# One step of a fused LSTM, attention, GRU and mixture-of-experts kernel laid out in another order

## The chip, the cores and the metric

The kernel runs on one core of a Trainium2 chip. The metric is the device time of one execution in microseconds (us). TensorE is called PE, VectorE DVE, ScalarE ACT, GpSimd POOL.

## The reference

Input x is 16 sequences of 128 time steps and 128 features. The result is x plus attention over an LSTM's output, and to that is added a mixture of experts over a GRU's output:

```python
x = x + attention(lstm(x, cond))      # causal softmax, 16 heads, rank-32 latents
x = x + experts(gru(x, cond))         # 8 experts of 512, top 2 of 8 by softmax

# LSTM step                           # GRU step
a = xw_t + h @ Wh                     z, r = sigmoid(comb @ Wz + bz), sigmoid(comb @ Wr + br)
c = f * c + i * g                     cand = tanh(concat(x_t, r * h) @ Wh + bh)
h = o * tanh(c)                       h = (1 - z) * h + z * cand
                                      # after every fourth step: h = tanh(h @ Wp + bp)
# experts
h = gelu(x @ w1 + b1); out_all = h @ w2 + b2     # exact gelu
out = sum of the two selected experts' rows, by their renormalised weights
```

Both recurrences are serial in time, 128 steps each. The attention is causal over time, so a block of 16 time steps can be attended to as soon as the LSTM has passed it. The GRU follows 29 steps behind the LSTM.

## The kernel before

The whole program is one loop over steps k, written out for each engine by hand. Step k holds LSTM step t = k and GRU step g = k - 29 (`LAG`), so both recurrences run in steps 29 to 127, only the LSTM before, only the GRU up to step 156, and after it what is left of the experts. Everything else is hung into fixed steps by their place modulo 16, which is called the phase below. Every engine works through its queue in the order in which the code stands, and semaphores tie the queues together.

In a step PE issues `g_step` (the two GRU gates into pG), `l_step` (four LSTM gates into pL), `g_candidate` (needs gRZ from DVE), and at the end of every fourth step `g_propagate`. ACT does tanh of each into gT, lT, gC, then lC, the tanh of the LSTM's cell. DVE makes gRZ and gA from gT, lP, oK and the cell (written to lT) from lT, then gB, ghi, g and glo (the GRU's new state, its high half and its low half), and hhi, hfull, hlo (the same for the LSTM). `l_fill` and `g_fill` put eight steps' input projections into pL and pG at once.

The attention of a block of 16 times is a visit of 8 units, each with two batch rows: `scores` at phase `O_S` plus the unit's number (13 small matmuls into pS, a single bank), then DVE's `maximum` (mx) and `subtract` (P), ACT's `exps` in place, `turn_probs` (transposes P into pV) at `O_T`, ACT's `pt_copy` (PTs), `values` at `O_V`, DVE's `normalise` and `turn_values`. `project` at two phases (`O_P`) closes each half block. `lat_q` makes latents and queries of 8 time steps. POOL spreads the queries into qbd.

The experts' visit m covers 16 GRU steps in two token tiles of 128 (tg 0 and 1). `expert_up(m, e, cp)` is 6 matmuls into pH[cp], one bank for each half cp of the hidden columns; ACT's `activate` (gelu) empties it into hid, two instructions for each cp. `expert_down(m, e, tg)` is a bias matmul and 4 fp32 matmuls into pY, and DVE's `combine` adds it to acc. Each down waits for the combine of the one before it. Routing is `route_x` on PE, `route_first` on DVE, a tanh (th) on ACT in the same step, and `route_rest` (10 small DVE instructions) one step later. `keep_warm(n)` issues n matmuls of 512 columns on zeros: 4 a step before step 18, 2 a step up to step 44. Two queue orders matter most:

```python
if route_at(k) is not None:                       # ACT, end of step k
    act.wait_ge(r_low, 2 * m + tg + 1)
    A(th[:, :], low[:, :], ACT.Tanh, scale=0.5).then_inc(r_th, 1)
...
if n >= 2:                                        # PE, expert_up
    pe.wait_ge(gelu, 2 * (n - 1))                 # the same bank's gelu of the expert before
```

Of the kernel before, what the change touches and what calls it, by code (L numbers as in the profile page):

```python
# [8 lines left out]
GS = 8  # L9
# [13 lines left out]

LAG = 29
O_S, O_T, O_V = 2, 3, 4
O_P = (9, 12)
O_R = (5, 13)
LAST = T + LAG
E_STEP = (0, 0, 1, 2, 2, 3, 4, 4)
NHID = 8  # L30
WARM_END = LAG + TB
W1_STEP = (17, 18, 19, 20, 21, 22, 23, 25)
# [15 lines left out]
def route_at(k):  # L48
    for tg, o in enumerate(O_R):
        q, r = divmod(k - o, TB)  # L50
        if r == 0 and 2 <= q <= NBLK + 1:
            return q - 2, tg
    return None


def up_at(k):
    out = []
    for m in range(NBLK):
        for e in range(E):
            at = LAST + e if m == NBLK - 1 else TB * m + LAG + TB + E_STEP[e]  # L60
            if at == k:
                out += [(m, e, 0), (m, e, 1)]
    return out


def down_at(k):
    out = []
    for m in range(NBLK):
        for e in range(E):
            for tg in range(2):  # L70
                at = LAST + 1 + e if m == NBLK - 1 else TB * m + LAG + TB + 2 + 2 * e + tg
                if at == k:
                    out.append((m, e, tg))
    return out


STEPS = LAST + 1 + E


def build(nc, a, out):  # L80
# [8 lines left out]
    with ctx:  # L89
# [179 lines left out]
        sub_done = sem("sub_done")  # L269
# [46 lines left out]
        def _(sp):  # L316
# [20 lines left out]
            for m in range(NBLK):  # L337
                for tg in range(2):
                    sp.wait_ge(acc_done, 2 * (E * m + E - 1) + tg + 1)
                    row = (2 + 2 * m + tg) * TOK  # L340
                    sp.dma_start(out[row:row + TOK, :], acc[:, m % 3, tg, :]).then_inc(stored[2 * (m % 3) + tg], 16)
            for m in range(NBLK - 3, NBLK):
                for tg in range(2):
                    sp.wait_ge(stored[2 * (m % 3) + tg], 16 * (m // 3 + 1))

        @block.gpsimd
        def _(pool):
# [41 lines left out]
            def rank_experts(m, tg):  # L389
                n = 2 * m + tg  # L390
                pool.wait_ge(r_cmp, 2 * n + 1)
                pool.tensor_tensor(eq[:, :, :], eq[:, :, :], tri[:, :, :], ALU.mult).then_inc(r_rank, 1)  # L392
                pool.wait_ge(r_cmp, 2 * n + 2)
                pool.wait_ge(r_rank, 2 * n + 1)
                pool.tensor_tensor(gt[:, :, :], gt[:, :, :], eq[:, :, :], ALU.add).then_inc(r_rank, 1)
                pool.wait_ge(r_rank, 2 * n + 2)

            for k in range(STEPS):
                if k % GS == 0 and GS <= k <= T:
                    split_latents(k // GS - 1)  # L400
# [5 lines left out]
                if route_at(k) is not None:  # L406
                    rank_experts(*route_at(k))

        @block.tensor
        def _(pe):  # L410
# [18 lines left out]
            def before_c(k):  # L429
                nq = len([j for j in range(k) if j % GS == 0 and GS <= j <= T])  # L430
                npj = len([j for j in range(k) if half_at(j) is not None])
                nr = len([j for j in range(k) if route_at(j) is not None])
# [27 lines left out]
            def lat_q(G, k):  # L460
                hi, lo = (flat(t[:, GS * G + 1:GS * G + GS + 1, :]) for t in (hhi, hlo))
                pe.wait_ge(l_lo, GS * G + GS)
                if G == 0:
                    pe.wait_ge(set_kvd, 2)
                    pe.wait_ge(set_qk, 1)
                    pe.wait_ge(set_qklo, 1)
                if G:
                    pe.wait_ge(lat_done, G)
                before = len([j for j in range(k) if unit_at(j, O_S) is not None])
                if before:  # L470
                    pe.wait_ge(sub_done, before)
                mm(pS[:, 0:TOK], Wkvdhi[:, :], hi, start=True)
                mm(pS[:, 0:TOK], Wkvdhi[:, :], lo)
                mm(pS[:, 0:TOK], Wkvdlo[:, :], hi).then_inc(lat_mm, 1)
# [8 lines left out]
            def scores(n, k):  # L483
# [6 lines left out]
                pe.wait_ge(lat_done, min(k // GS, NG))  # L490
                if n:
                    pe.wait_ge(sub_done, n)
# [9 lines left out]
            def turn_probs(n):  # L502
                pe.wait_ge(exp_done, n + 1)
# [543 lines left out]
```

## Time and profile before

| | |
|---|---|
| three runs | 729.1, 722.74, 728.73 us (median 728.73) |
| profiled execution | 724.37 us, of it 722.6 us span |
| PE, DVE, ACT, POOL busy | 86%, 58%, 41%, 19% |
| PE's granted clock, mean | 0.898 |
| chain that ended last | PE 64%, DVE 18%, ACT 10%, issue 6% |

PE is the engine that is most busy, but its matmuls overlap and their ends are modelled, so 86% does not say that PE is full; the chain says for what share of the time something else was what the end waited for. The clock tells what share of full speed (2.4 GHz) PE was granted; 1.2 GHz shows as 0.5.

### The profile page before, as it was taken

How to read it: one execution, taken by the hardware profiler on the slowest of the kernel's cores; microseconds unless marked ns; L12 is line 12 of the kernel's file. 1: busy time of each engine (PE TensorE's matmuls, PEld its weight loads, DVE VectorE, ACT ScalarE, POOL GpSimd, SP SyncE). 2: the span in 40 equal slices, each digit the busy share in tenths (PEclk: the TensorE clock that was granted, in tenths of full speed). 3: DMA queues.
4: the chain of work that ended last, by engine and by line, in shares of the span. 5: the costliest groups of instructions: out<-in, count | busy, mean ns of one | idle time of the engine just before them, and what ended most of it. 6: DMA issues, size and time to landing. Idle time of an engine off the chain costs nothing.

```text
span 722.6 us, 18818 instructions
## 1 busy us (share of the span) xinstructions
PE 623.3 (86%) x6952; PEld 550.6 (76%) x6952; DVE 420.9 (58%) x2372; ACT 293.4 (41%) x1004; POOL 134.3 (19%) x339
## 2 busy tenths in 40 slices
PE   5988889988899888898898889888988888877898
PEld 2656767876788878887888778877888688766787
DVE  2476656664586558655776478655875476435321
ACT  1354323235532464245422653355434532451143
POOL 4006204200331024102320043003310231000000
PEclk8795785599988999999979999999999999998599
DMA  9400000000000000000000000000000000000000
GB/s 257 176 1 1 2 1 1 3 1 1 2 3 1 5 5 3 2 5 5 3 1 2 8 3 3 1 10 1 2 2 5 6 1 2 4 6 2 0 8 9
DMA packets 5528, 10.03 MB, mean 14 GB/s; under 512 B 1827, under 2 KB 4527, under 8 KB 5054
## 3 DMA queue, kind: packets, MB, share of 16 engines
q1 hardware_dynamic: 4686, 6.47, 2.5%
q10 hardware_dynamic: 752, 2.37, 1.3%
q8 instruction: 56, 0.92, 0.6%
q14 instruction: 34, 0.28, 0.1%
HBM read 7.79 MB, written 1.05 MB: 12 GB/s over the span
## 4 chain that ended last, share of the span: by engine, by line
PE 64%; DVE 18%; ACT 10%; issue 6%; DMA 1%; SPq 0%; POOL 0%; DVEq 0%; POOLq 0%
PE pY L412 18%; PE pG L412 11%; PE pH L412 10%; PE pV L412 8%; PE pL L412 6%; PE pV L507 4%; ACT hid L746 4%; PE pS L412 3%; PE pC L412 3%; ACT PTs L736 2%; DVE acc L940 1%; DMA lWx<-in_lWx 1%; DVE gRZ L949 1%; DVE ghi L965 1%; DVE mx L858 1%
## 5 line engine op out<-in xcount | busy, mean ns | idle before, releaser
L412 PE MATMUL pY<-w,hid 128*128 128x128 f32 x1024 | 155.3, 299 | 0.0
L412 PEld LDWEIGHTS pY<-w,hid 128*128 128x128 f32 x1024 | 136.3, 207 | 0.1
L746 ACT ACTIVATE hid<-pH,b 128x256 f32<-128x256 f32 x256 | 105.6, 471 | 63.0 <-PE pH L412 61.6
L385 POOL COPY qbd<-qh 32x256 f16<-32x256 f16 x256 | 104.3, 408 | 141.5 <-PE pS L412 127.8
L949 DVE SCALAR_TENSOR_TENSOR gRZ<-gT,g 128x32 f32<-128x32 f32 x128 | 26.8, 210 | 115.4 <-ACT gT L754 115.2
L412 PE MATMUL pG<-gRZ,gW 128*128 128x16 f32 x256 | 51.1, 276 | 36.5 <-DVE gRZ L949 36.4
L412 PE MATMUL pV<-latN,PTs 128*128 128x33 f32 x512 | 76.8, 298 | 6.6 <-ACT PTs L736 6.6
L736 ACT ACTIVATE PTs<-pV 128x512 f32<-128x512 f32 x64 | 38.2, 597 | 107.6 <-PE pV L507 107.6
L412 PEld LDWEIGHTS pG<-gRZ,gW 128*128 128x128 f32 x256 | 42.8, 210 | 46.1 <-DVE gRZ L949 45.3
L412 PEld LDWEIGHTS pV<-latN,PTs 128*128 128x128 f32 x512 | 70.1, 212 | 9.4 <-ACT PTs L736 8.6
L412 PE MATMUL pH<-ghi,w1hi 128*128 128x256 f16 x256 | 70.6, 276 | 6.6 <-ACT hid L746 5.5
L412 PE MATMUL pH<-glo,w1hi 128*128 128x256 f16 x256 | 70.8, 277 | 0.0
L412 PE MATMUL pH<-ghi,w1lo 128*128 128x256 f16 x256 | 70.7, 276 | 0.0
L940 DVE SCALAR_TENSOR_TENSOR acc<-pY,gates,acc 128x128 f32<-128x128 f32 x128 | 44.4, 347 | 33.6 <-PE pY L412 32.4
L962 DVE TENSOR_TENSOR gB<-gRZ,gC 128x16 f32<-128x16 f32 x128 | 24.2, 189 | 61.6 <-ACT gC L764 60.9
L764 ACT ACTIVATE gC<-pG 128x16 f32<-128x16 f32 x128 | 23.3, 182 | 81.8 <-PE pG L412 81.6
L754 ACT ACTIVATE gT<-pG 128x32 f32<-128x32 f32 x128 | 24.8, 194 | 70.5 <-PE pG L412 70.5
L412 PE MATMUL pY<-still 128*128 128x512 bf16 x138 | 48.8, 476 | 1.2 <-DVE still L786 1.2
L392 POOL TENSOR_TENSOR eq<-eq,tri 128x64 f32<-128x64 f32 x16 | 5.1, 318 | 238.1 <-DVE gt L904 238.1
L507 PE MATMUL pV<-ident,P 128*128 128x128 f32 x256 | 46.5, 312 | 2.5 <-DVE On L874 2.5
L412 PE MATMUL pL<-hhi,lWhi 128*128 128x16 f16 x512 | 41.8, 171 | 4.4 <-DVE hhi L969 4.4
L412 PEld LDWEIGHTS pL<-hhi,lWhi 128*128 128x128 f16 x512 | 35.2, 102 | 13.1 <-DVE hhi L969 11.0
(155 smaller groups left out, 1448.3 us busy)
## 6 DMA issues: line engine op xcount, KB each, us to landing
w<-in_w SPq DMA_DIRECT2D x2, 2048.0 KB, 10.8
out<-acc SPq DMA_DIRECT2D x16, 64.0 KB, 1.5
xT<-in_xT ACTq DMA_DIRECT2D x1, 960.0 KB, 10.4
hid<-in_WqT ACTq DMA_DIRECT2D x1, 512.0 KB, 5.6
hid<-in_Wout ACTq DMA_DIRECT2D x1, 512.0 KB, 7.9
lWh<-in_lWh SPq DMA_DIRECT2D x1, 256.0 KB, 2.8
lWx<-in_lWx SPq DMA_DIRECT2D x1, 256.0 KB, 9.5
gWh<-in_gWh SPq DMA_DIRECT2D x1, 192.0 KB, 7.5
```

The costliest lines, as they stand in the source:

```text
L385: pool.tensor_copy(qbd[r, n % 2, :, :, q, :], qh[r, p % 2, :, 2 * u:2 * u + 2, :, :].rearrange("p l b (g c) t -> p l (b g) (c t)", g=2)).t ...
L412: return nc.tensor.matmul(o, lhsT=lhsT, rhs=rhs, start=start, stop=stop, skip_group_check=True)
L507: last = nc.tensor.transpose(pV[:, 128 * j:128 * (j + 1)], P[:, n % 3, j, :], ident[:, :])
L736: A(PTs[:, n % 2, :, :].rearrange("p j q -> p (j q)"), pV[:, :], ACT.Copy).then_inc(pt_done, 1)
L746: A(hid[:, e % NHID, 2 * cp + c, :], pH[cp][:, 256 * c:256 * (c + 1)], ACT.Gelu, bias=b1[:, e, 2 * cp + c:2 * cp + c + 1], scale=1.0 / SP) ...
L754: A(gT[:, :, :], pG[:, 0:2, g % GS, :], ACT.Tanh, scale=1.0 / SP).then_inc(g_tanh, 1)
L764: A(gC[:, :], pG[:, 2, g % GS, :], ACT.Tanh, scale=1.0 / SP).then_inc(g_c, 1)
L858: V.tensor_reduce(mx[:, :], S_of(keys(n // NU)), AX.X, ALU.max).then_inc(mx_done, 1)
L940: V.scalar_tensor_tensor(acc[:, m % 3, tg, :], pY[:, D * tg:D * (tg + 1)], gates[:, m % 2, tg, e:e + 1], acc[:, m % 3, tg, :], ALU.mult, A ...
L949: V.scalar_tensor_tensor(gRZ[:, :, :], gT[:, :, :], 1.0, g8[:, at:last + 1:last - at, :], ALU.add, ALU.mult).then_inc(g_rh, 1)
L962: V.tensor_tensor(gB[:, :], gRZ[:, 1, :], gC[:, :], ALU.mult).then_inc(g_b, 1)
L965: V.scalar_tensor_tensor(ghi[:, g, :], gA[:, :], keep, gB[:, :], ALU.mult, ALU.add).then_inc(g_hi, 1)
```

## The change

- The step's order. PE now issues `g_step`, a first slot of other work (A: `values`, the second `project`, `lat_q` at phase 0, a down), `g_candidate`, then `l_step`, then a second slot (B) with everything else, and `scores` last of all. ACT and DVE follow: lT, lC, lP, oK and the cell come behind gC and behind glo.
- The exp. `subtract` is gone; `maximum` gives the negated maximum and moves one step later, ahead of gB. The exp reads pS directly with the maximum as its bias, one instruction for each of the four blocks, two of them ahead of lC and two behind it. `O_S` goes from 2 to 1, and the next unit's scores wait for all four exps, where they waited for the subtraction.
- The experts. Visits now cover tiles 2m-1 and 2m, so there are nine, the first and the last of one tile. Up matmuls are one expert a step at phases 10 to 15, 0 and 1, both cp in the step, and their gelus follow one step later, cp 0 between gT and gC, cp 1 behind lC. Downs stand in the table `DOWNS`, up to three in a group with one wait for the group.
- The routing on DVE is cut in four (`route_first`, `route_soft`, `route_pick`, `route_gates`, the last three 2, 3 and 4 steps after `route_x`), and ACT's th moves to the end of the following step.
- `keep_warm` writes to pH[1], with 4 a step up to step 28 and 2 + 2 a step in 29 to 41. Latents go to a quarter of pY, not to pS.

```diff
-O_S, O_T, O_V = 2, 3, 4
+O_S, O_T, O_V = 1, 3, 4
-E_STEP = (0, 0, 1, 2, 2, 3, 4, 4)
-WARM_END = LAG + TB
+NVIS = NBLK + 1
+WARM_END = 42
+TAIL = 149
+UPS = tuple(42 + e for e in range(E))
+DOWNS = ((45, "A", (0, 0)), (46, "A", (0, 1)), (47, "A", (1, 0)), (49, "A", (1, 1)), (49, "B", (2, 0)),
...
+def up_step(m, e):
+    return LAST + e if m == NVIS - 1 else TB * NBLK + 37 - TB + e if m == NVIS - 2 else TB * m + UPS[e]
...
             def scores(n):
-                    pe.wait_ge(sub_done, n)
+                    pe.wait_ge(exp_done, 4 * n)
...
+            def experts_down(group):
+                for at, (m, e, tg) in enumerate(group):
+                    n = ORDER[(m, e, tg)]
+                    pe.wait_ge(gelu, 4 * (E * m + e + 1))
...
+                    elif at == 0:
+                        pe.wait_ge(acc_done, n)
...
             for k in range(STEPS):      # PE
                 if 0 <= g < T:
                     g_step(g)
+                if unit_at(k, O_V) is not None:
+                    values(unit_at(k, O_V))
+                if half_at(k) is not None and k % TB == O_P[1]:
+                    project(half_at(k), k)
+                if latents_at(k) is not None and k % TB == 0:
+                    lat_q(latents_at(k), k)
+                if (k, "A") in DOWN_AT:
+                    experts_down(DOWN_AT[(k, "A")])
+                if LAG <= k < WARM_END:
+                    keep_warm(k, 2)
+                if 0 <= g < T:
+                    g_candidate(g)
                 if t < T:
                     l_step(t)
...
+                for m, e in UP_AT.get(k, []):
+                    expert_up(m, e, 0)
...
+                for m, e in UP_AT.get(k, []):
+                    expert_up(m, e, 1)
...
+                if unit_at(k, O_S) is not None:
+                    scores(unit_at(k, O_S))
+                if k < WARM_END:
+                    keep_warm(k, 0 if k in (1, 2) else 2 if k >= LAG else 4)
...
+            def exps(n, pair):          # ACT
+                act.wait_ge(mx_done, n + 1)
+                for j in (2 * pair, 2 * pair + 1):
+                    A(P[:, n % 3, j, 0:L], S_of(L)[:, j, :], ACT.Exp, bias=mx[:, j:j + 1]).then_inc(exp_done, 1)
...
+                for m, e in UP_AT.get(k - 1, []):
+                    activate(m, e, 0)
                 if 0 <= g < T:
                     act.wait_ge(g_cand, g + 1)
...
+                if unit_at(k - 1, O_S) is not None:
+                    exps(unit_at(k - 1, O_S), 0)
...
+                if unit_at(k - 1, O_S) is not None:
+                    exps(unit_at(k - 1, O_S), 1)
+                for m, e in UP_AT.get(k - 1, []):
+                    activate(m, e, 1)
```

ACT's queue where an attention visit begins. Before, one load of the exp's table (L730) stands ahead of the first exp, between lT and gC:

```order
L754 ACTIVATE gT<-pG 128x32
L757 ACTIVATE lT<-pL 128x64
L730 ACT_TABLE_LOAD
L730 ACTIVATE P<-P 128x4x64
L764 ACTIVATE gC<-pG 128x16
L767 ACTIVATE lC<-lT 128x16
```

Now, in steps of phase 2 and 3, with the last expert's gelu (hid) between the exps (P):

```order
L781 ACT_TABLE_LOAD
L781 ACTIVATE P<-pS,mx 128x64 x2
L818 ACTIVATE lC<-lT 128x16
L781 ACTIVATE P<-pS,mx 128x64 x2
L798 ACT_TABLE_LOAD
L798 ACTIVATE hid<-pH,b 128x256 x2
L805 ACTIVATE gT<-pG 128x32
L810 ACTIVATE gC<-pG 128x16
L813 ACTIVATE lT<-pL 128x64
L781 ACT_TABLE_LOAD
L781 ACTIVATE P<-pS,mx 128x64 x2
```

There are two loads more in each visit that overlaps an expert visit: 26 in the program where there were 14.

DVE's queue in a step of phase 5 (attention in full course). Before, the LSTM's cell (lP, oK, lT) stood ahead of the normalisation (rs, On) and of the GRU's update (gB to glo):

```order
L949 SCALAR_TENSOR_TENSOR gRZ<-gT,g 128x32
L951 SCALAR_TENSOR_TENSOR gA<-gT,g 128x16
L954 SCALAR_TENSOR_TENSOR lP<-lT 128x32
L955 TENSOR_SCALAR oK<-lT 128x16
L957 SCALAR_TENSOR_TENSOR lT<-lP 128x16
L872 RECIPROCAL rs<-pV 128x4
L874 TENSOR_TENSOR On<-pV,rs 128x128
L962 TENSOR_TENSOR gB<-gRZ,gC 128x16
L965 SCALAR_TENSOR_TENSOR ghi<-gA,gB 128x16
L966 SCALAR_TENSOR_TENSOR g<-gA,gB 128x16
L969 TENSOR_TENSOR hhi<-oK,lC 128x16
```

Now the combine (acc) and the maximum (mx) of the step before come ahead of gB, and the cell comes behind all of them:

```order
L1003 SCALAR_TENSOR_TENSOR gA<-gT,g 128x16
L992 SCALAR_TENSOR_TENSOR acc<-pY,gates,acc 128x128
L913 TENSOR_REDUCE mx<-pS 128x4
L1010 TENSOR_TENSOR gB<-gRZ,gC 128x16
L1013 SCALAR_TENSOR_TENSOR ghi<-gA,gB 128x16
L1014 SCALAR_TENSOR_TENSOR g<-gA,gB 128x16
L1016 TENSOR_TENSOR glo<-g,ghi 128x16
L917 RECIPROCAL rs<-pV 128x4
L919 TENSOR_TENSOR On<-pV,rs 128x128
L1023 SCALAR_TENSOR_TENSOR lP<-lT 128x32
L1024 TENSOR_SCALAR oK<-lT 128x16
L1026 SCALAR_TENSOR_TENSOR lT<-lP 128x16
```

The cell, on which ACT's lC waits, moved from the fifth place in the step to the thirteenth.

## Rows read from the trace of the kernel before

**Rows 1.** Stretches: length; busy PE, PEld, DVE, ACT, POOL; granted clock; DMA.

```profile
55.90:99.00 43.10, 37.87 (x401) 31.57 (x402) 26.25 (x122) 15.19 (x47) 14.49 (x31) 0.72 0.01 2
99.00:166.90 67.90, 61.55 (x638) 51.05 (x635) 41.26 (x261) 19.75 (x87) 14.83 (x38) 0.67 0.01 2
166.90:259.40 92.50, 81.71 (x992) 74.21 (x989) 55.80 (x346) 45.24 (x156) 16.21 (x42) 0.93 0.01 3
259.40:335.60 76.20, 66.08 (x853) 61.37 (x849) 49.38 (x293) 34.45 (x123) 15.41 (x40) 0.98 0.01 4
335.60:626.10 290.50, 253.17 (x3028) 236.07 (x3025) 189.05 (x1034) 125.81 (x427) 60.14 (x156) 0.96 0.01 3
626.10:682.60 56.50, 44.69 (x365) 39.93 (x362) 22.97 (x137) 19.85 (x68) 1.27 (x4) 0.82 0.01 4
682.60:722.60 40.00, 34.23 (x272) 30.24 (x272) 10.24 (x42) 13.89 (x35) 0.64 (x2) 0.92 0.03 8
```

**Rows 2.** Groups by line and form, 259.4 to 335.6 us: busy, mean ns.

```profile
L746 ACT ACTIVATE hid<-pH,b 128x256 f32<-128x256 f32 x32 | 13.2, 472 | 6.3 <-PE pH L412 6.0
...
L940 DVE SCALAR_TENSOR_TENSOR acc<-pY,gates,acc 128x128 f32<-128x128 f32 x16 | 5.5, 346 | 0.1
...
L757 ACT ACTIVATE lT<-pL 128x64 f32<-128x64 f32 x16 | 3.6, 225 | 0.9
...
L867 DVE TENSOR_TENSOR P<-pS,mx 128x256 f32<-128x256 f32 x8 | 3.4, 424 | 0.3
...
L858 DVE TENSOR_REDUCE mx<-pS 128x4 f32<-128x256 f32 x8 | 3.3, 413 | 0.0
```

**Rows 3.** Timeline of step 147, GRU only: start, length, engine, line.

```profile
652.18 0.20 ACT L754 ACTIVATE gT<-pG 128x32 f32<-128x32 f32 x1 [1.01 <-PE pG L412]
...
652.66 0.39 PE L412 MATMUL pG<-gRZ,gW 128*128 128x16 f32 x2 [0.51 <-DVE gRZ L949]
...
653.09 0.18 ACT L764 ACTIVATE gC<-pG 128x16 f32<-128x16 f32 x1 [0.71 <-PE pG L412]
653.31 0.18 DVE L962 TENSOR_TENSOR gB<-gRZ,gC 128x16 f32<-128x16 f32 x1 [0.62 <-ACT gC L764]
...
653.81 0.17 DVE L973 TENSOR_TENSOR glo<-g,ghi 128x16 f16<-128x16 f32 x1
...
654.29 0.20 ACT L754 ACTIVATE gT<-pG 128x32 f32<-128x32 f32 x1 [1.01 <-PE pG L412]
```

**Rows 4.** Timeline of ACT in step 77, phase 13: a table load before gelu.

```profile
320.66 1.28 ACT L746 ACT_TABLE_LOAD   x1
...
321.96 0.84 ACT L746 ACTIVATE hid<-pH,b 128x256 f32<-128x256 f32 x2
...
322.69 0.18 ACT L764 ACTIVATE gC<-pG 128x16 f32<-128x16 f32 x1
```

**Rows 5.** The chain of waits in order of time: pieces of steps 68 and 69.

```profile
277.98 0.39 PE pS L412 x13
...
282.00 0.93 PE pV L412 x8
```

**Rows 6.** The chain of waits at the end: ups (x6) and downs (x9).

```profile
709.97 0.66 PE pH L412 x6
710.62 1.04 PE pY L412 x9
...
720.21 0.35 DVE acc L940
```

**Rows 7.** Timeline at the end of step 69: ACT's th, and gT behind it.

```profile
286.64 0.21 ACT L778 ACTIVATE th<-low 128x8 f32<-128x8 f32 x1 [1.05 <-DVE low L906]
...
286.76 0.18 ACT L754 ACTIVATE gT<-pG 128x32 f32<-128x32 f32 x1
```

**Rows 8.** Timeline of step 67: DVE beside POOL's copies.

```profile
274.46 1.81 POOL L385 COPY qbd<-qh 32x256 f16<-32x256 f16 x4 [1.33 <-PE pS L412]
...
274.91 0.41 DVE L962 TENSOR_TENSOR gB<-gRZ,gC 128x16 f32<-128x16 f32 x1 [1.03 <-ACT gC L764]
```

More of the change, by code:

```diff
@@ L335, in _ @@
                 sp.dma_start(whole(t), a[name]).then_inc(loaded_moe, 16)
-            for m in range(NBLK):
-                for tg in range(2):
[L339 to L344, printed above, removed]
+            for i in range(NG):
+                m, tg = visit_of(i)
+                sp.wait_ge(acc_done, ORDER[(m, E - 1, tg)] + 1)
+                row = (2 + i) * TOK
+                sp.dma_start(out[row:row + TOK, :], acc[:, m % 3, tg, :]).then_inc(stored[2 * (m % 3) + tg], 16)
+            for m in range(NVIS - 3, NVIS):
+                for tg in range(2):
+                    used = slots_used(m, tg) + (tg < len(tiles_of(m)))
+                    if used:
+                        sp.wait_ge(stored[2 * (m % 3) + tg], 16 * used)
         @block.gpsimd
@@ L398, in _ @@
             for k in range(STEPS):
-                if k % GS == 0 and GS <= k <= T:
-                    split_latents(k // GS - 1)
+                if latents_at(k) is not None:
+                    split_latents(latents_at(k))
                 n = unit_at(k, O_S)
@@ L429, in before_c @@
             def before_c(k):
-                nq = len([j for j in range(k) if j % GS == 0 and GS <= j <= T])
+                nq = len([j for j in range(k) if latents_at(j) is not None])
                 npj = len([j for j in range(k) if half_at(j) is not None])
-                nr = len([j for j in range(k) if route_at(j) is not None])
+                nr = len([j for j in range(k) if j in ROUTES])
                 bank_c(nq, npj, nr)
@@ L466, in lat_q @@
                     pe.wait_ge(set_qklo, 1)
+                n = len([d for (at, slot), ds in DOWN_AT.items() if at < k for d in ds])
                 if G:
                     pe.wait_ge(lat_done, G)
[L469 to L474, printed above, removed]
+                if n:
+                    pe.wait_ge(acc_done, n)
+                M = pY[:, 3 * TOK:4 * TOK]
+                mm(M, Wkvdhi[:, :], hi, start=True)
+                mm(M, Wkvdhi[:, :], lo)
+                mm(M, Wkvdlo[:, :], hi).then_inc(lat_mm, 1)
                 before_c(k)
@@ L481, in lat_q, with scores @@
                 last.then_inc(q_mm, 1)
-            def scores(n, k):
+            def scores(n):
                 p, u = divmod(n, NU)
@@ L620, in _ @@
-                if 0 <= g < T:
-                    g_candidate(g)
-                if k % GS == 0 and GS <= k <= T:
-                    lat_q(k // GS - 1, k)
-                if unit_at(k, O_S) is not None:
-                    scores(unit_at(k, O_S), k)
-                while ups or downs:
-                    if downs:
-                        expert_down(*downs.pop(0))
-                    if ups:
-                        expert_up(*ups.pop(0))
                 if unit_at(k, O_T) is not None:
@@ L781, in _ @@
                     A(gp, pG[:, 3, (g + 1) % GS, :], ACT.Tanh, scale=1.0 / SP).then_inc(g_p, 1)
+                if unit_at(k, O_T) is not None:
+                    pt_copy(unit_at(k, O_T))
+                if latents_at(k) is not None:
+                    q_copy(latents_at(k))
+                if k - 1 in ROUTES:
+                    n = ROUTES[k - 1]
+                    act.wait_ge(r_low, n + 1)
+                    A(th[:, :], low[:, :], ACT.Tanh, scale=0.5).then_inc(r_th, 1)
         @block.vector
```

307 lines of the change are left out of this document (156 added, 151 removed).

## The prediction, made before the changed kernel was run

> **What bounds the kernel now.** I read the stretches first [rows 1], then one bare step [rows 3], then the single pieces. Between 166.9 and 626.1 us lie steps 45 to 140, 96 steps in 459.2 us (92.5 + 76.2 + 290.5), so 76.5 us for 16 steps or 4.8 a step; that is where the time is. A step with only the GRU and one down takes 2.11 us from gT to gT [rows 3], and PE's own work in 16 steps comes to about 61 us from the pieces: an expert with both tiles is 2 x 0.66 up and 2 x 1.0 down, so 26.6 for eight; a unit 0.39 for scores, 0.93 for values [rows 5] and 0.45 for transposes, so 14.2 for eight; the recurrences' own matmuls about 0.7 a step, 11; latents, projections and fills about 9. So some 15 of 76 us are latency: an engine's queue stands behind an instruction that waits. PE "busy" 66.1 of 76.2 [rows 1] hides this. The question is not how much work is left but which waits each step holds in the new order.
>
> **Unit costs.** From the bare step [rows 3], with gT's start as 0: the candidate's matmul at 0.48, gC 0.43 after it, gB 0.22 after gC, glo 0.50 after gB, and the next gT 0.48 after glo (0.35 after the first matmul of `g_step`). DVE's small instructions start 0.1 apart where independent and 0.2 where one feeds the next. A pair of gelus is 0.84 (two of 0.47 overlapping [rows 2, 4]). A table load is 1.28, and the gelu starts 0.02 behind it [rows 4].
>
> **A step with experts (phases 11 to 15, 0, 1), new order.** The down in slot A ends 0.75 after gT, so the candidate is at 0.75, gC 1.18, gB 1.40, glo 1.90, lP 2.0, cell 2.2, lC 2.4. Only then comes gelu cp 1, 2.5 to 3.35. Up cp 1 of the next expert uses the same bank and waits: 3.5 to 4.15 (0.66 [rows 6]). `g_step` is queued behind it: gT at 4.5. So 4.5 us for one expert a step, PE idle about 1.2 of it. Phase 15 adds `l_fill` behind that up (a 512-column bias and four fp32 matmuls, about 1.1 at a down's 0.24 each [rows 6]): 5.6. Phases 12 and 0 have the propagation, whose next gate matmuls are fp32 (+0.3), and an early wait for x1: 5.05 and 4.7. Phase 1 adds scores 0.4 and a down that waits for its combine: 5.1. Phase 11 has the table load ahead of gelu cp 0, and so ahead of gC: 6.05.
>
> **A step with attention (phases 4 to 8).** Values end 0.7 after gT, gC 1.15, gB 1.37 (combine 0.35 and maximum 0.41 [rows 2] are over by 1.1, so they are hidden), glo 1.87, rs and On to 2.46, cell 2.6, lC 2.8, second exp pair 2.9 to 3.43, scores 3.55 to 3.9, gT 4.26. Adding the exps: an exp of 64 from PSUM without a bias would be as lT, 0.225; with one it goes by gelu's 0.472 for 256 [rows 2], less 192 elements at the 0.83 ns that 64 to 256 cost at least, 0.31. I take 0.31, since gelu also carries a bias pointer; the pair is 0.53, and the low end 0.35 would save 0.18 in each of seven steps. What goes is the subtraction, 0.424 on DVE [rows 2], but it lay where DVE had time. Results: phase 4 is PE's own 4.7 (with `g_fill`), 5 to 7 are 4.3, 8 is 4.6, and 9 and 10 (q_rest and routing push gRZ late, `pt_copy` pushes values) 4.7 and 4.6.
>
> The Trainium skill, ScalarE: Activation LUTs, What ACT_TABLE_LOAD costs, gives an ACTIVATE with a bias pointer as 280 ns and 0.833 ns an element, 0.33 for 64. The gelu row, 0.472 against 0.493 by that rule, agrees within 5%; the sum would be longer by 0.3 us in 16 steps.
>
> **The loads.** The queue order shows two more a visit. Phase 2: gT, gelus, gC, lT to 1.3, load to 2.6, exps, lC 3.0, exps to 3.7, load to 5.0, gelu cp 1 to 5.8, gT 5.7 where the same phase took 2.6 before. Phase 3: its load runs while DVE does three combines and the maximum, the exps wait for it, 4.65. Twelve loads more are 15.4 us on ACT at 1.28 [rows 4]; about 2.5 of each visit's 2.6 ends up in the steps' length.
>
> The same section of the Trainium skill gives 1283 ns for the load and 1380 ns for a drain, 2.66 us a switch, and its rule is to batch calls by set, which speaks against this change. The load's row agrees, the drain's does not: the gelu starts 0.02 us after the load's end. By the page twelve switches would be 31.9 us, by the row 15.4.
>
> **What improves.** ACT's th stood directly ahead of gT [rows 7], with the whole routing on DVE ahead of it; it cost about 0.8 us twice in 16 steps. Two experts in one step with a load (phase 13, 5.9 us before) becomes 4.5. Phases 5 to 7 gain up to 1 us each.
>
> **The sum for 16 steps.** Phases 0 to 15: 4.7, 5.1, 5.7, 4.65, 4.7, 4.3, 4.3, 4.3, 4.6, 4.7, 4.6, 6.05, 5.05, 4.5, 4.5, 5.6 = 77.3. The same count on six phases of before (3, 4, 5, 10, 11, 12) gives 24.5 where the trace has 25.7, because DVE stretches beside POOL's copies (gB 0.41 for 0.18 [rows 8]) and semaphores take time; with that 5% it is 81.2. Before has 77.1 for the five such periods (steps 45 to 124) and 73.6 for the sixth, of which the most is without the LSTM.
>
> **The whole, against the profiled span of 722.6:**
> - Steps 0 to 17: same chain, 0.
> - Steps 18 to 28, 43.1 us at clock 0.72 [rows 1]: the two further warm-up matmuls keep it high, as four did before step 18; a step is then about 3.9 (values 0.93, l_step and lT 0.5, lC 0.7, exps and scores 1, warm-up 0.86) for 4.7. Sum 37: -6. If the clock stays low, +7 instead.
> - Steps 29 to 44, 67.9 us at 0.67: high clock, but the LSTM's half of DVE now runs behind the GRU's, and four warm-up matmuls (0.86) lie on the path: 70, +2.
> - Five periods: 5 x (81.2 - 77.1) = +20.5; longer key rows with the block's number +5 (before holds them already); the first expert visit has one tile, -7. Sixth period 70 for 73.6, -4. Together +15.
> - Steps 141 to 155: 57 for 56.5 (626.1 to 682.6), +1.
> - After: 40.0 us before, 16 downs at 0.66 + 1.04 each [rows 6] behind the routing of the last tiles. Now the last visit has one tile: step 156 3.9, three grouped steps 3, 3 and 4.1, seven experts at 1.7, and 2.4 to the end: 28.4, -11.5.
>
> Sum -6 + 2 + 15 + 1 - 11.5 = +0.5: a span of 723, a time of 725. That execution lies below the median of the three (724.4 and 728.7), so I say **724 us**, the change a trade that comes out about even.
>
> **The rivals.**
> - Faster: the new order's waits overlap better than a chain worked out step by step says (gelu cp 1 slips ahead, exps at 0.35 a pair, no stretch beside POOL), so that a period comes near 75. Then 6 x 6 less: 724 - 36 = 688, and with half of it 706. For it: PE's own 61 us, and the balance of the phases, 3.0 to 4.7 of PE's work in each. Against: lC is last on a queue of DVE that I cannot shorten, and before, the same count was too short, not too long. Chance 0.33, at 680 to 714.
> - Slower: the exps as gate of the recurrence. Scores of a unit wait for the exps behind lC and `g_step` is queued behind the scores, so in seven steps of 16 every stretch on DVE between gRZ and the cell (13 instructions) is on the path. If they stretch like gB [rows 8] in half of the cases, that is 0.6 a step, 4.2 a period, 25 in all: 749. It decides from a phase 5 of over 4.9 us. For it: POOL's copies fall in just these phases (15.4 us of 76.2 [rows 1]). Chance 0.22, at 736 to 760.
> - The clock: PE idles 1.2 us in most steps and the granted clock falls more often than before (0.93 to 0.98 in this stretch [rows 1]). 30 us more at 1.2 GHz cost about 12: 736. Chance 0.1.
> - Forecast 0.35, at 714 to 736.
>
> **How the numbers follow.** Within 1% is about what a measurement of this kernel can tell from no change: 721.4 to 736.0 by the median. Of the forecast's 0.35 some 0.09 lie below and 0.01 above. Faster 0.33 + 0.09 = 0.42; the same 0.25 and a few hundredths of the clock's case, 0.28; slower the rest, 0.30. The range that leaves out 2 in 10 is 690 to 750; the forecast's own is 714 to 736.
>
> **What would show it.** Phases 13 and 14 at 4.5 us with up cp 1 waiting for the gelu; phase 2 near 5.7 with 26 loads in all; phases 5 to 7 at 4.3 to 4.6, scores waiting for exp; phase 11 over 5.5; after the last gT 28 us; clock near 1 in steps 18 to 44. I am wrong if phases 11 to 15 run below 4 us (then the gelu is not the gate) or if phases 4 to 8 run above 5.

## Result and profile after

| | before | after |
|---|---|---|
| median, lowest to highest | 728.91 us (722.74 to 732.34) | 855.91 us (853.5 to 860.1) |
| profiled execution, its span | 724.37, 722.6 us | 853.5, 851.6 us |
| PE's granted clock, mean | 0.898 | 0.836 |

The change makes the kernel 17.6% slower: the ratio is 1.176 [1.167, 1.185]. Forecast were 724 us and a range of 690 to 750. Totals go by medians; the profiled executions of the kernels in experiments 1, 6 and 9 ran longer (806 us for 794, 773 for 767, 771 for 749) and at a lower clock than their other runs.

The page of the changed kernel: busy time, the granted clock in 40 slices, shares of the chain, and two groups (busy, mean ns, then PE's idle time in front of them and what ended it).

```profile
PE 679.1 (80%) x7090; PEld 603.3 (71%) x7090; DVE 398.2 (47%) x2308; ACT 354.2 (42%) x1240; POOL 131.5 (15%) x339
...
PEclk8886966665667998789977998789977998599999
...
PE 63%; DVE 16%; ACT 13%; issue 6%; DMA 1%; SPq 0%; POOL 0%; DVEq 0%; POOLq 0%; ACTq 0%
...
L538 PE MATMUL pV<-ident,P 128*128 128x128 f32 x256 | 59.8, 378 | 68.1 <-DVE On L919 66.4
...
L443 PE MATMUL pH<-ghi,w1hi 128*128 128x256 f16 (+1 forms) x288 | 77.1, 273 | 43.5 <-ACT hid L798 42.7
```

The same two groups before, in the view by line:

```profile
L412 PE MATMUL pH<-ghi,w1hi 128*128 128x256 f16 x256 | 70.6, 276 | 6.6 <-ACT hid L746 5.5
...
L507 PE MATMUL pV<-ident,P 128*128 128x128 f32 x256 | 46.5, 312 | 2.5 <-DVE On L874 2.5
```

The chain's shares have hardly moved. What has moved are two of PE's waits: the transposes of P stood 2.5 us behind DVE's On, now 66.4, and the ups 5.5 us behind the gelu, now 42.7. Besides, the transposes take 378 ns for 312, a sign of the clock.

The stretches after (length; busy PE, PEld, DVE, ACT, POOL; clock; DMA), for [rows 1]: steps 18 to 28, 29 to 44, 45 to 124, 141 to 155 and the rest; behind them phases 5 to 11 of steps 64 to 79 alone.

```profile
60.20:105.20 45.00, 39.33 (x404) 30.07 (x404) 22.78 (x112) 18.45 (x72) 9.38 (x25) 0.78 0.01 2
105.20:192.50 87.30, 70.40 (x691) 56.94 (x690) 39.24 (x253) 28.31 (x121) 14.86 (x38) 0.67 0.01 1
192.50:669.40 476.90, 377.00 (x4150) 353.26 (x4150) 238.07 (x1417) 212.87 (x741) 77.04 (x200) 0.84 0.01 3
760.40:822.20 61.80, 52.45 (x493) 47.37 (x491) 24.60 (x146) 23.78 (x83) 1.33 (x4) 1.00 0.01 2
822.20:851.60 29.40, 24.36 (x258) 23.05 (x257) 8.53 (x39) 12.74 (x43) 0.64 (x2) 1.00 0.04 11
...
330.60:378.10 47.50, 38.72 (x378) 36.54 (x379) 22.89 (x137) 16.82 (x63) 5.79 (x15) 0.75 0.01 3
```

Before, steps 45 to 124 took 385.6 us at a clock of 0.96; now they take 476.9 at 0.84. Of 129.0 us more of span, 91 are there, 19 in steps 29 to 44 and 17 in steps 125 to 140.

Step 69 (phase 5), which the forecast put at 4.3 us and which takes 6.19:

```profile
330.59 0.20 ACT L805 ACTIVATE gT<-pG 128x32 f32<-128x32 f32 x1 [0.22 <-PE pG L443]
...
331.76 0.24 PE L443 MATMUL pL<-hlo,lWhi 128*128 128x16 f16 x4
...
332.78 0.29 DVE L919 TENSOR_TENSOR On<-pV,rs 128x128 f32<-128x128 f32 x1
...
333.21 1.09 PE L538 MATMUL pV<-ident,P 128*128 128x128 f32 x4 [1.20 <-DVE On L919]
333.41 0.22 ACT L818 ACTIVATE lC<-lT 128x16 f32<-128x16 f32 x1 [0.73 <-DVE lT L1026]
...
334.20 2.02 PE L443 MATMUL pY<-w,hid 128*128 128x128 f32 x8
...
336.78 0.20 ACT L805 ACTIVATE gT<-pG 128x32 f32<-128x32 f32 x1 [1.84 <-PE pG L443]
```

`turn_probs` waits for `on_done`, because the transposes write to pV, the bank in which `values` left what On reads. Before, the transposes came late in PE's step. Now they stand directly behind `l_step`, and On stands on DVE behind combine, maximum and gB to glo. PE stops for 1.20 us, and the down, the scores and the next `g_step` stop with it. Then the down takes 2.02 us, against 1.04 [rows 6]: PE is at 1.2 GHz from 332.7 to 336.1. The LSTM's lC is long done by then, so what the forecast took for the path, glo to cell to lC to the exps, is not what the end of this step waits for.

### The profile page after: what moved, and what is told of

The parts are those of the page before. It is cut to its first block, busy times and chain, and to the rows that moved or that the text cites. A ratio compares the mean times of both kernels' runs of the same rounds, so it can differ in the third digit from the quotient of the medians.

```text
span 851.6 us, 19294 instructions
## 1 busy us (share of the span) xinstructions
PE 679.1 (80%) x7090; PEld 603.3 (71%) x7090; DVE 398.2 (47%) x2308; ACT 354.2 (42%) x1240; POOL 131.5 (15%) x339
## 4 chain that ended last, share of the span: by engine, by line
PE 63%; DVE 16%; ACT 13%; issue 6%; DMA 1%; SPq 0%; POOL 0%; DVEq 0%; POOLq 0%; ACTq 0%
PE pY L443 16%; PE pH L443 13%; PE pG L443 9%; PE pV L538 7%; PE pV L443 6%; ACT hid L798 5%; PE pL L443 5%; PE pC L443 5%; PE pS L443 4%; DVE gB L1010 2%; DVE On L919 2%; ACT L798 2%; ACT gC L810 2%; DVE ghi L1013 2%; DVE glo L1016 2%
## 5 line engine op out<-in xcount | busy, mean ns | idle before, releaser
L443 PEld LDWEIGHTS pY<-w,hid 128*128 128x128 f32 x1024 | 146.5, 220 | 2.3
L798 ACT ACTIVATE hid<-pH,b 128x256 f32<-128x256 f32 (+1 forms) x288 | 111.9, 445 | 12.0 <-PE pH L443 11.8
L538 PE MATMUL pV<-ident,P 128*128 128x128 f32 x256 | 59.8, 378 | 68.1 <-DVE On L919 66.4
L443 PE MATMUL pH<-ghi,w1hi 128*128 128x256 f16 (+1 forms) x288 | 77.1, 273 | 43.5 <-ACT hid L798 42.7
L538 PEld LDWEIGHTS pV<-ident,P 128*128 128x128 f32 x256 | 39.1, 190 | 71.9 <-ACT P L781 59.4
L443 PE MATMUL pH<-ghi,w1lo 128*128 128x256 f16 (+1 forms) x288 | 78.0, 276 | 0.0
L443 PE MATMUL pH<-glo,w1hi 128*128 128x256 f16 (+1 forms) x288 | 77.9, 276 | 0.0
L443 PEld LDWEIGHTS pH<-ghi,w1hi 128*128 128x128 f16 x288 | 29.9, 104 | 53.3 <-issue 49.6
L781 ACT ACTIVATE P<-pS,mx 128x16 f32<-128x16 f32 (+7 forms) x256 | 66.0, 315 | 1.2 <-DVE mx L913 0.6
L818 ACT ACTIVATE lC<-lT 128x16 f32<-128x16 f32 x128 | 27.6, 216 | 90.3 <-DVE lT L1026 89.3
```

What stands on the lines that cost most here:

```text
L443: return nc.tensor.matmul(o, lhsT=lhsT, rhs=rhs, start=start, stop=stop, skip_group_check=True)
L538: last = nc.tensor.transpose(pV[:, 128 * j:128 * (j + 1)], P[:, n % 3, j, :], ident[:, :])
L781: A(P[:, n % 3, j, 0:L], S_of(L)[:, j, :], ACT.Exp, bias=mx[:, j:j + 1]).then_inc(exp_done, 1)
L798: A(hid[:, e % NHID, 2 * cp + c, 0:W], pH[cp][:, 256 * c:256 * c + W], ACT.Gelu, bias=b1[:, e, 2 * cp + c:2 * cp + c + 1], scale=1.0 / SP) ...
L818: A(lC[:, :], lT[:, 4, :], ACT.Tanh, scale=0.5).then_inc(l_tc, 1)
```

## Experiments

Times are medians. The kernel before took 731 to 734 us beside these runs and 728.9 beside the changed kernel, which was not run again, so differences to its 855.9 are uncertain by some 5 us. "Half clock" is the time at 1.2 GHz in steps 45 to 124 of the profiled execution: 34 us before, 157 after.

**1. The transposes moved back behind the downs.** Changed kernel, PE's queue only.

```diff
-                if unit_at(k, O_T) is not None:
-                    turn_probs(unit_at(k, O_T))
                 for m, e in UP_AT.get(k, []):
 ...
                     experts_down(DOWN_AT[(k, "B")])
+                if unit_at(k, O_T) is not None:
+                    turn_probs(unit_at(k, O_T))
```

> The changed kernel with one move: the four transposes of P stand on PE behind the downs of slot B instead of directly behind l_step. Theory A: the transposes wait for On (1.2 to 1.4 us of PE standing still in each step of phases 4 to 10), everything in slot B is queued behind them, and the idle stretch also lets the granted clock fall, so that the down behind it takes 1.9 us for 1.0. Then both go: phases 5 to 7 fall from 6.2 - 6.9 us to 4.3 - 4.9, the granted clock in these phases is near 1, and the time is 770 to 790 us for 856. Rival B: the clock is low for another reason (PE stands still behind the gelus as well), and only the wait's own 0.5 us a step goes: 825 to 840 us. Rival C: transposes that come later make pt_copy and the next step's values late, and nothing is gained.

Measured: 793.6 us (785.1 to 806.3), ratio to before 1.079 [1.070, 1.089], so 62 us less than the changed kernel, a little short of theory A's 770 to 790. Step 69:

```profile
314.45 0.20 ACT L805 ACTIVATE gT<-pG 128x32 f32<-128x32 f32 x1 [0.22 <-PE pG L443]
...
315.78 1.11 PE L443 MATMUL pY<-w,hid 128*128 128x128 f32 x8
...
317.07 0.63 PE L538 MATMUL pV<-ident,P 128*128 128x128 f32 x4 [0.18 <-DVE On L919]
...
318.75 0.20 ACT L805 ACTIVATE gT<-pG 128x32 f32<-128x32 f32 x1 [0.37 <-PE pG L443]
```

The down covers the wait for On, the clock is at 2.4 GHz, and the step takes 4.29 us, the 4.3 of the forecast. Steps 18 to 28 take 39.9 us. But PE's wait for On is 20.8 us in all, phases 7 to 10 still run at half clock in part (4.4 to 8.1 us a step), and half clock is 144 us in the profiled execution. So most of the wait goes here, but from step 64 on only phases 5 and 6 are free of half clock throughout.

**2. On moved ahead of gB.** The same wait, taken from its other end: PE's queue as in the changed kernel, on DVE the normalisation behind the maximum.

```diff
                     maximum(unit_at(k - 1, O_S))
+                if unit_at(k, O_V) is not None:
+                    normalise(unit_at(k, O_V))
 ...
-                if unit_at(k, O_V) is not None:
-                    normalise(unit_at(k, O_V))
```

> The changed kernel with one thing moved on DVE: rs and On (the normalisation) stand behind the maximum and ahead of gB, where they stood behind glo. PE's queue is untouched: the transposes still stand directly behind l_step. It is the same wait as in the kernel with the transposes moved behind the downs (793.6 us), taken from its other end. Theory (the transposes wait for On, and the clock falls with the stall): in a step of phase 5 the values end about 0.9 us after gT, rs and On then take 0.45, so On is over at about 1.5 in place of 2.5 and the transposes wait 0.2 to 0.4 us in place of 1.2; gB comes 0.1 to 0.3 later. Phases 5 to 8 fall from 6.2 to 6.9 us to 4.5 to 5, half clock in steps 45 to 124 falls below 100 us from 157, and the whole is at 785 to 815. Rival 1 (it was not the wait but the place: the gain of the moved transposes came from the downs going ahead of them): the time stays within 10 us of 856. Rival 2 (gB behind On is on the recurrence's path and the clock stays low): 840 to 870, with PE's wait on On gone from the chain but phases 5 to 8 above 6.

Measured: 767.8 us (762.3 to 768.1), 1.047 [1.039, 1.055]: 88 us less than the changed kernel, more than the theory's 785 to 815. Both rivals fall. Step 69, then the wait by line, then phases 5 to 11:

```profile
308.06 0.20 ACT L805 ACTIVATE gT<-pG 128x32 f32<-128x32 f32 x1 [0.22 <-PE pG L443]
...
309.34 0.29 DVE L919 TENSOR_TENSOR On<-pV,rs 128x128 f32<-128x128 f32 x1
...
309.78 0.63 PE L538 MATMUL pV<-ident,P 128*128 128x128 f32 x4 [0.30 <-DVE On L919]
...
310.30 1.11 PE L443 MATMUL pY<-w,hid 128*128 128x128 f32 x8
```

```profile
L538 PE MATMUL pV<-ident,P 128*128 128x128 f32 x256 | 46.1, 309 | 20.2 <-DVE On L919 16.6 <-ACT P L781 3.5
```

```profile
308.06:340.03 31.97, 28.18 (x376) 26.76 (x378) 22.47 (x137) 16.07 (x62) 5.89 (x15) 1.00 0.01 4
```

The wait is 16.6 us for 66.4, the down is back at 1.11 for 2.02, phases 5 to 8 take 4.0 to 4.8 us from step 64 on (but for one of 5.7, at half clock), and the seven phases 5 to 11 take 32.0 us at 2.4 GHz where they took 47.5 at 0.75. Half clock is 68 us. That gB comes later costs nothing that shows. PE's wait is 50 us shorter, and 88 us came back. Which part of them is the clock's, this experiment can't say, since wait and clock went together.

**3. The wait kept, PE kept busy in it.** Changed kernel, five matmuls of 512 columns on zeros ahead of the transposes in phases 4 to 10 (the wait on gelu keeps them off a bank in use).

```diff
                 if unit_at(k, O_T) is not None:
+                    if k % TB > O_T and k >= 52:
+                        pe.wait_ge(gelu, 4 * E * min((k - 42) // TB + (1 if (k - 42) % TB >= 8 else 0), NVIS - 2))
+                        keep_warm(k, 5)
                     turn_probs(unit_at(k, O_T))
```

> The changed kernel with five matmuls of 512 columns on zeros (0.216 us each at full clock, 1.1 together) ahead of the transposes in phases 4 to 10, from step 52 on. The wait for On stays, only PE is busy while it lasts. If the idle stretch is what brings the clock down (theory A), the clock in these phases stays near 1 and phases 5 to 7 fall from 6.2 - 6.9 us to about 4.8 - 5.2; the time is 795 to 815 us. If the clock does not depend on it (B), the ten half-clock matmuls' worth of 2.2 us per step is longer than the wait, and the kernel gets slower by about 0.8 us in 40 steps: 885 us or more.

Measured: 798.8 us (795.5 to 802.7), 1.091 [1.083, 1.098], 57 us less, with more work in the queue and On where it was. Step 69, then the same seven phases:

```profile
323.99 0.20 ACT L808 ACTIVATE gT<-pG 128x32 f32<-128x32 f32 x1 [0.22 <-PE pG L443]
...
325.26 1.24 PE L443 MATMUL pH<-still 128*128 128x512 bf16 x5
...
326.61 0.63 PE L538 MATMUL pV<-ident,P 128*128 128x128 f32 x4
...
327.13 1.11 PE L443 MATMUL pY<-w,hid 128*128 128x128 f32 x8
```

```profile
324.00:361.80 37.80, 34.42 (x407) 28.72 (x408) 22.88 (x137) 16.36 (x62) 5.78 (x15) 1.00 0.01 3
```

The transposes start 2.62 us behind gT, exactly as in the changed kernel, but they take 0.63 us for 1.09 and the down 1.11 for 2.02, so the step takes 4.80 us for 6.19. The seven phases take 37.8 us at 1.00, for 47.5 at 0.75 in the changed kernel and 32.0 with the wait gone: of those 15.5 us, 9.7 come with the clock and the other 5.8 with the wait and whatever the filler adds. Half clock is 48 us. This shows the clock's part as a cause of its own, and that PE's idle time in the stall brings it about.

**4. The loads.** Ups one step earlier: 14 table loads where the changed kernel has 26. Then the same together with experiment 1.

```diff
-UPS = tuple(42 + e for e in range(E))
+UPS = tuple(41 + e for e in range(E))
```

> The changed kernel with the ups of every visit but the last two one step earlier (phases 9 to 0 instead of 10 to 1), so that the last gelu is done before the first exp: 14 table loads for 26. If the two loads a visit are what phases 2 and 3 pay (5.8 and 4.6 to 6.0 us), phase 2 falls to about 4.3 and the time by 15 to 25 us, to 832 to 841. If they lie under the downs anyway, no change: 850 to 860.

> Both edits, transposes behind the downs and ups one step earlier. If the two causes are independent the savings add: theory A gives 750 to 772 us, B 810 to 825. A rest of 20 us or more above the kernel before (729) then belongs to the gelu of the second bank, which comes behind lC and holds back the next up and g_step (phases 13 and 14 at 4.46 us for 4.65 on average over the two before).

Measured: 851.5 us (848.1 to 866.9), 1.162 [1.151, 1.174]; with experiment 1, 789.2 (788.0 to 791.3), 1.078 [1.071, 1.084]. That is 4 us each time (beside the changed kernel, within the 5 us of uncertainty), not 15 to 25. Phase 2 does fall in two periods of five (4.8 and 4.9 us for 5.9), but takes 6.4 to 7.5 in the other three, at half clock, and phase 9, which now holds an up behind a stall at half clock, rises to 8.1 to 9.4 from 6.6 to 7.1. So I had the price of the loads right at their place and wrong in sum. Phase 2 of the changed kernel, as forecast:

```profile
314.99 0.22 ACT L813 ACTIVATE lT<-pL 128x64 f32<-128x64 f32 x1
315.23 1.28 ACT L781 ACT_TABLE_LOAD   x1
316.52 0.52 ACT L781 ACTIVATE P<-pS,mx 128x64 f32<-128x64 f32 x2
316.93 0.21 ACT L818 ACTIVATE lC<-lT 128x16 f32<-128x16 f32 x1
...
317.57 1.28 ACT L798 ACT_TABLE_LOAD   x1
318.86 0.84 ACT L798 ACTIVATE hid<-pH,b 128x256 f32<-128x256 f32 x2
319.59 0.20 ACT L805 ACTIVATE gT<-pG 128x32 f32<-128x32 f32 x1
```

**5. The gelu of cp 1 ahead of lC.** The kernel with both of 1 and 4; this gelu stands directly behind lT.

```diff
                     A(lT[:, 0:4, :], pL[:, :, t % GS, :], ACT.Tanh, scale=1.0 / SP).then_inc(l_tanh, 1)
+                for m, e in UP_AT.get(k - 1, []):
+                    activate(m, e, 1)
 ...
-                for m, e in UP_AT.get(k - 1, []):
-                    activate(m, e, 1)
                 setup(k)
```

> The kernel of the last experiment (transposes behind the downs, ups one step earlier) with one more move on ACT: the gelu of the second bank (cp 1) stands directly behind lT, ahead of lC, where it stood behind lC. Theory: this gelu is what holds the next expert's up, and with it g_step; it then ends at 2.2 us after gT instead of 3.4, and phases 12 to 0 fall by about 1 us each (13 and 14 from 4.46 to 3.4 - 3.6), seven steps of 16, so 35 to 50 us in all: 740 to 755 us for 789. Rival: lC, which now waits behind the gelu or behind DVE's cell as before, makes hhi and so gRZ of the next step late, and phases 13 and 14 stay above 4.1; then 775 or more.

Measured: 752.4 us (748.8 to 767.8), 1.024 [1.018, 1.030], 37 less than without. The changed kernel in phase 13 first, then this one:

```profile
382.99 0.20 ACT L805 ACTIVATE gT<-pG 128x32 f32<-128x32 f32 x1 [1.09 <-PE pG L443]
...
385.37 0.22 ACT L818 ACTIVATE lC<-lT 128x16 f32<-128x16 f32 x1 [0.72 <-DVE lT L1026]
385.49 0.82 ACT L798 ACTIVATE hid<-pH,b 128x256 f32<-128x256 f32 x2
...
386.45 0.27 PE L443 MATMUL pH<-ghi,w1hi 128*128 128x256 f16 x1 [1.40 <-ACT hid L798]
...
387.44 0.20 ACT L805 ACTIVATE gT<-pG 128x32 f32<-128x32 f32 x1 [1.13 <-PE pG L443]
```

```profile
338.61 0.20 ACT L805 ACTIVATE gT<-pG 128x32 f32<-128x32 f32 x1 [0.83 <-PE pG L443]
...
340.16 0.83 ACT L798 ACTIVATE hid<-pH,b 128x256 f32<-128x256 f32 x2
340.99 0.22 ACT L820 ACTIVATE lC<-lT 128x16 f32<-128x16 f32 x1
341.14 0.27 PE L443 MATMUL pH<-ghi,w1hi 128*128 128x256 f16 x1 [0.46 <-ACT hid L798]
...
342.12 0.20 ACT L805 ACTIVATE gT<-pG 128x32 f32<-128x32 f32 x1 [0.92 <-PE pG L443]
```

Phases 13 and 14 take 3.52 us for 4.46. Against the kernel without this move, the ups' wait for hid falls from 46.0 to 18.2 us (the downs' wait for hid rises from 4.1 to 11.4), and half clock from 104 to 72 us. In this order the gelu, through the up's bank, gates `g_step`, as the forecast said.

**6. More filler.** The kernel of 5 with four zero matmuls ahead of the scores in phases 2 to 8.

```diff
                 if unit_at(k, O_S) is not None:
+                    if k >= 50 and k % TB >= 2:
+                        pe.wait_ge(gelu, 4 * E * ((k - 34) // TB))
+                        keep_warm(k, 4)
                     scores(unit_at(k, O_S))
```

> The previous kernel with four matmuls of 512 columns on zeros ahead of the scores in phases 2 to 8, where PE waits about 1 us for the exps. If the granted clock is what is left (104 us at 1.2 GHz in steps 45 to 124 of the kernel before it, 34 in the kernel before the change), these phases lose their half-clock stretches and 20 to 35 us go, to 710 to 730 us, the level of the kernel before the change or better. If the filler lies on the path instead, each phase grows by up to 0.9 us and the time by up to 30.

Measured: 766.9 us (761.0 to 773.4), 1.043 [1.036, 1.050], 14.5 slower, though half clock fell from 72 to 44 us. Here, where the long stall is gone, filler costs more than the clock gives back.

**7. The routing's tanh late, in the kernel before.** Here, in 8 and 9 and in the first half of 10 one part of the change alone goes into the old order. th stands at the end of the next step, behind everything that gT needs, and the rest of the routing on DVE comes one step later too.

```diff
-                if route_at(k) is not None:
-                    m, tg = route_at(k)
                 if 0 <= g < T - 1 and g % 4 == 3:
 ...
+                if route_at(k if k == LAST else k - 1) is not None and k != LAST + 1:
+                    m, tg = route_at(k if k == LAST else k - 1)
 ...
```

> The kernel before with one part of the change alone: ACT's th of the routing at the end of the next step instead of directly ahead of the next gT, and the rest of the routing on DVE one step later. The prediction puts about 0.8 us on that wait, twice in 16 steps: 10 to 14 us less, 715 to 722 for 729. If the wait was hidden (PE busy until then), no change; if gT's place is taken by the next instruction in line (gelus in phase 13), 3 to 6 us less.

Measured: 713.2 us (711.6 to 721.1), 0.976 [0.968, 0.983]. The gain is 20 us where I expected 10 to 14. Step 69 took 5.01 us and takes 3.74: gT comes directly behind pt_copy, with no th ahead of it as in [rows 7]. Half clock falls to 17 us, which may be why it is more than the wait.

```profile
280.87 0.60 ACT L736 ACTIVATE PTs<-pV 128x512 f32<-128x512 f32 x1 [1.54 <-PE pV L507]
281.37 0.19 ACT L754 ACTIVATE gT<-pG 128x32 f32<-128x32 f32 x1
```

**8. The exp from PSUM, in the kernel before.** No subtraction; four exps with the maximum as bias, at the old place.

```diff
-                A(P[:, n % 3, :, 0:L], P[:, n % 3, :, 0:L], ACT.Exp).then_inc(exp_done, 1)
+                for j in range(4):
+                    A(P[:, n % 3, j, 0:L], S_of(L)[:, j, :], ACT.Exp, bias=mx[:, j:j + 1]).then_inc(exp_done, 1)
 ...
```

> The kernel before with another part alone: no subtraction, the maximum negated, and the exp in four instructions that read the scores' bank with the maximum as bias, at the old place between lT and gC; scores wait for the exps where they waited for the subtraction. By the prediction's prices 0.42 us goes from DVE and four exps of 0.31 (about 0.95 as a row of four, for 0.42) stand ahead of gC: the gain on DVE lies at a step's end, the 0.5 us on ACT lies on the way to gC in 7 of 16 steps, so 0 to 20 us slower, 729 to 750. If this part were a cause of the 127 us of the whole change, it would have to cost 40 or more.

Measured: 744.7 us (742.0 to 758.1), 1.014 [1.007, 1.020]. By itself this part costs 11 us. An exp of 64 with bias takes 0.328 us:

```profile
L734 ACT ACTIVATE P<-pS,mx 128x64 f32<-128x64 f32 x32 | 7.4, 328 | 0.0
```

**9. The transposes early, in the kernel before.** `turn_probs` directly behind `g_candidate`, all else as it was.

> The cause put into the kernel before: the transposes of P directly behind the candidate, where they wait for On, with scores and the down queued behind them, and nothing else changed. By the count on DVE, On ends 1.8 us after gT and the transposes are reached at 1.15, so PE stands still 0.7 us in phases 4 to 10 (1.2 to 1.4 in the changed kernel). If such a stretch alone brings the clock down, these phases get 0.5 to 1.4 us longer and the time is 755 to 790 us; if only the wait counts, 730 to 745; if 0.7 us is hidden in the 15 us of latency of a period, 725 to 735.

Measured: 748.9 us (747.6 to 770.6) beside 731.1, between the ranges of the expectation. Of the six runs of the kernel before beside it, one took 717.8 us and five 729.1 to 741.5. The wait for On is 22.0 us for 2.5:

```profile
L507 PE MATMUL pV<-ident,P 128*128 128x128 f32 x256 | 50.5, 331 | 28.6 <-DVE On L874 22.0
```

So the wait costs in the old order too: 18 us by the medians, 31 against the one run of 717.8. That is less than in the new order, and On is earlier on DVE there. The other half, On backward on DVE in the old order, was not run.

**10. The warm-up.** Once the kernel of 7 with four warm-up matmuls a step up to step 28 (they were two from step 18), once the kernel of 5 with the warm-up as it was before.

```diff
-                if k < 18:
+                if k < LAG:
                     keep_warm(0 if k in (1, 2) else 4)
```

> The kernel before with the later th (713 us) and four warm-up matmuls a step up to step 28, where it had two from step 18 on. The prediction put 6 us on this part: steps 18 to 28 (43 to 46 us at a clock of about 0.7) at full clock would take 37. So 705 to 710 us if the clock follows; 714 to 720 if it stays low and the 22 matmuls only add to the steps.

> The best version of the changed kernel (752 us) with the warm-up of the kernel before: two matmuls a step from step 18 on and none in slot A of steps 29 to 41. Steps 29 to 44 take 81 us there and 68 in the kernel before; if the 52 matmuls on the path (0.22 us each, 0.43 at half clock) are the reason, 8 to 13 us of it goes and the time is 738 to 745; if the order of the step is (the LSTM's half of DVE behind the GRU's) or the clock falls further, 750 to 760.

Measured: 705.6 us (700.8 to 711.6), 0.965 of the 731.1 beside it (717.8 to 741.5; 0.98 of the fastest of those), with steps 18 to 28 at 39.1 us for the 46.4 of experiment 7. Its slowest run is faster than every run of either kernel. The other one took 760.4 us (757.1 to 767.3), 8 more than in 5, with steps 29 to 44 at 81.3 us for 80.7: taking the warm-up matmuls out doesn't shorten that stretch, which then has 55 us at half clock for 44.

## Why the prediction was wrong

**The step that failed** is "a step with attention (phases 4 to 8)", and with it phases 9 and 10, which hold the same transposes. It followed ACT's and DVE's path (glo, cell, lC, second exp pair, scores) and let PE's queue run beside it: it never asked what `turn_probs` waits for. These seven phases were forecast at 31.5 us a period (33 with the 5%) and took 47.2 in steps 68 to 74. The forecast named its own sign, "if phases 4 to 8 run above 5"; from step 64 on they ran at 6.2 to 7.1. Its rival "exps as gate" gave the same sign for another reason, and experiment 2 excludes that one as the cause: the exps stayed where they are, and phases 5 to 8 went down to 4.0 to 4.8 us (phase 4 to 5.5 to 5.8, still above its 4.7, and why is open). That rival's own sum is too low as well: 13 instructions, half of them 0.23 us longer, make 1.5 us a step and not 0.6. The exp from PSUM has a price of its own, 11 us in the old order.

**The clock** was a rival at 0.10 with 30 us more at half speed, for 12 us. It was 123 us more in steps 45 to 124. That PE's waits can cost clock was right, where they do was not: "PE idles 1.2 us in most steps" counted the gelu's wait in the expert phases, and phases 12 to 15 ran at full clock with it from step 76 on, while the stall in phases 4 to 10, which the forecast did not have, brought 3.4 us at half clock into every step of phases 5 to 10 from step 64 on. Experiment 3, which leaves the wait and fills it, gave 57 us back, and 9.7 of 15.5 us in the seven phases. The difference between the 88 us of experiment 2 and its 50 us less of wait, 38, is smaller than these 57, so waits and clock don't simply add.

**Where it came.** The span was 129 us above the forecast's 723: 73 in steps 45 to 124 (476.9 for 404), 21 in steps 125 to 140 (91.0 for 70), 17 in steps 29 to 44 (87.3 for 70), 8 in steps 18 to 28 (44.9 for 37), and some 10 in the rest.

**What held.** Measured against forecast, in us, from step 64 on: phases 13 and 14 4.46 for 4.5; 12 4.93 for 5.05; 15 5.57 for 5.6; 11 5.97 for 6.05 (6.65 in one period); 0 4.57 for 4.7; 2 5.8 to 6.0 for 5.7. Phase 1 missed with 5.7 to 5.9 for 5.1, and phase 3 with 4.6 to 6.1 for 4.65. The tail is 29.4 for 28.4.

With the wait gone (experiment 2), steps 80 to 95 take 81.2 us, which is the forecast period to the tenth. That match is luck in part: 3 and 9 take 5.9 and 6.6 for 4.65 and 4.7, and phases 5 to 8 less than the 5% allowance gave them. Steps 45 to 124 are then 409.5 us for 404, and steps 29 to 44 69.9 for 70.

**What was wrong beside it**, in experiment 2, which came to a span of 760 for 723: steps 0 to 17, from the first lT, 45.5 us for 38.1 ("same chain, 0"; step 15 takes 3.6 us for 2.3 and step 17 5.3 for 2.3; scores now begin at phase 1, in one step with the latents, which may be why); steps 18 to 28 48.3 for 37, with 30 us of them at half clock (in experiment 1, with 6 us at half clock, steps 19 to 22 take 3.87, where 3.9 was forecast, and the stretch still 39.9); steps 125 to 140 77.9 for 70, 141 to 155 61.9 for 57. Together 32 of the 37 us. The changed kernel itself has 44.9 us in steps 18 to 28, between the 37 and the 50 given for a high and a low clock.

**The parts.** The routing's tanh was forecast at "about 0.8 us twice in 16 steps", some 10 us, and gives 20 together with the later routing on DVE. The twelve loads were forecast at 2.5 us a visit and net 4 us in all when taken out, since the ups that replace them at phase 9 meet the stall. The exp's 0.31 us was 0.328; the Trainium skill, ScalarE: Activation LUTs, What ACT_TABLE_LOAD costs, gives 0.333 by its rule, and experiment 8 agrees within 2%. Its drain of 1.38 us a switch has no place in phase 2 above: each load is 1.28 us, and the exp or the gelu starts 0.01 us behind it.

**Open.** Why steps 29 to 44 take 80.7 us with the transposes late (5) and 69.9 with On early (2) was not tried apart; the clock there is at half speed for 44 and 20.5 us, which argues for the clock, no more. The same holds for 3 and 9 in experiment 2. What makes phase 1 longer than forecast was not looked for. The kernel with both On early and the gelu of experiment 5 was not run.

## What to carry to other kernels

Before an instruction is moved forward in an engine's queue, list every semaphore that it waits for, the one that frees its output's bank too, and look up where the releaser now stands on its own engine: here a transpose went forward on PE and the read of its bank went backward on DVE. The first move alone cost some 18 us in the old order; taking back either one in the new order returned 62 and 88. The Trainium skill, PSUM — Partial Sum Buffer, PSUM bank collisions raise a hardware error, has the rule to guard PSUM by bank. Here the transposes also overwrite the columns that On reads (0 to 255 of pV), so the guard would be needed without that rule; in this order it is a wait of 66.4 us. Where the granted clock falls with a stall of PE, price the stall well above its length, 88 us for 50 here, and look at the clock of the stretch first, since the waits for the gelu cost no clock. And where a large relayout holds several parts, time them one by one: one of the smallest, a tanh and the routing behind it moved by one step, was the one that paid most.

## What the hardware showed

A stall of 1.2 us in each step of about 6 was enough to bring the granted clock to 0.75 over seven steps in which PE shows 38.7 of 47.5 us busy. In the same steps 0.2 to 0.3 us left it at 1.00 (other steps of that kernel, phases 3 and 9 among them, still had 3.4 us at half clock), and so did a stall of the same length filled with zero matmuls. The length of the stall doesn't decide alone. Right behind these steps, phases 12 to 15 of the changed kernel stay at 1.00 with waits of 1.11 to 1.40 us for the gelu in steps of 4.46 to 5.57 and a smaller busy share, 15.0 of 19.4 us:

```profile
378.10:397.50 19.40, 14.99 (x186) 13.45 (x186) 8.65 (x59) 9.37 (x35) 0.64 (x2) 1.00 0.02 4
```

What sets the two cases apart was not tested. The slower clock then makes the step behind the stall longer: a down takes 2.02 us for 1.11, and the transposes 1.09 for 0.63.
